# Attention and FFN kernel: whole turns at a unit's end in the last head, edge column and square on ScalarE, key product in score banks, last block closed in halves

## The chip, the cores and the metric

The kernel runs on one core of one Trainium2 chip. The metric is device time in microseconds (us) of one execution. The kernel before was run three times: 1582.94 us in the median, 1581.42 to 1584.07. Engines are named as in the profile: PE (TensorE), DVE (VectorE), ACT (ScalarE), POOL (GpSimd) and SP (SyncE), which here only issues DMAs.

## The reference

The input is x of shape (2, 2048, 256), fp32. There are two stages, each followed by a residual and a layer norm.

```python
q, k, v = x @ Wq + bq, x @ Wk + bk, x @ Wv + bv          # 16 heads of 16, q and k rotated
probs = softmax(q @ k.T / sqrt(16))                      # 2 x 16 heads, 2048 x 2048
x = layernorm(x + probs @ v)

x_prev = x shifted by one token (zero at the start of a sequence)
xr = mu_r * x + (1 - mu_r) * x_prev
xk = mu_k * x + (1 - mu_k) * x_prev
out = sigmoid(xr @ W_r.T) * (square(relu(xk @ W_k.T)) @ W_v.T)
x = layernorm(x + out)
```

## The kernel before, in words

Every engine has its own program, written out by hand; semaphores order them. There is no scheduler: an instruction stands on its engine where the code puts it, and waits there for the semaphore counts that the code names.

**Attention.** The 32 pairs of batch and head (called heads here, 0 to 31) are worked one after the other by `period(h)`, each in 16 units `kt` of 128 keys. In a unit PE writes four score tiles of 128 keys by 512 queries (L543, each as four matmuls of 32 columns) into three PSUM banks `score_ps` used in turn, ACT takes the exponential of each (L696), and at the unit's end PE multiplies the four tiles of the unit before with the values (`pv`, L479) into the bank `pv_ps`. Score tile n waits until the exponential of tile n-3 is done. In the heads before the last, PE also computes the scores of the head after for its maxima (L446), and DVE reduces these (L931). The last head, 31, has no such work beside it.

**Beside the last head.** Three blocks of 512 tokens of batch 0 are prepared for the FFN while head 31 runs: DVE normalises them (`normalise`, L966), PE turns each from tokens to channels (`turn`, 8 transposes of 128 x 128, L491), DVE copies the turned block out of PSUM, sets the edge column for the shift by one token and multiplies with 1 - mu (`take_turned`), and mixes (`mix`, L1003). `project_r(0)` is eight matmuls of 128 x 256 (L503). In `period(LAST)` the iterator `stage_c`, fed by `beside(kt)`, gives one of these PE instructions after each score tile: turns start at units 5, 7 and 14, the r product at unit 10, there after every second tile.

**FFN.** Eight blocks n of 512 tokens. PE's order for a block is: turn of block n+1 (from n = 2 on), `project_r(n)`, `value(n-1)`, `project_key(n)`. PE's first instruction after the last head, `project_key(0)`, stands behind a wait for `pv_turned`, since its second bank is `pv_ps`, which DVE has to read first (`turn_context`, L941). ACT does the turned copy (`take_turned`, L715), the multiplication with 1 - mu (L721), the sigmoid (L727) and the relu (L734). DVE does the edge column (`edge`, L978, or L975 where the sequence starts), the mix, the square of the relu (`square`, L1011), the gating and the residual (`finish`, L1018 and L1021, in two halves), and the statistics (`block_stats`, L957, L960). POOL computes 1/sqrt(variance + eps) (`inverse`, L858, L861) and normalises the output of blocks 0 to 5 (L874); DVE normalises blocks 6 and 7 at the end (L1084), and SP stores each block by one DMA of 512 KB (L401).

The banks: `ring_ps` is two double banks, one for turns (`turn_ps`), one for r (`r_ps`). `key_ps` is `score_ps[2]` and `pv_ps`, `value_ps` is `score_ps[0]` and `score_ps[1]`.

The order around the change is set by DVE's and ACT's in-order programs: the edge column of block n+1 stands on DVE behind the gating, square, statistics and normalisation of the iteration before, ACT's multiplication waits for it, and DVE's mix waits for ACT.

## Time and profile before

| what | value |
|---|---|
| median of three runs | 1582.94 us |
| time of the profiled execution | 1584.12 us |
| its span | 1582.3 us |
| PE busy | 1545.5 us (98%) |
| DVE busy | 1345.3 us (85%) |
| ACT busy | 1139.0 us (72%) |
| POOL busy | 335.3 us (21%) |
| granted PE clock, mean | 0.993 |

The profiled execution took 1584.12 us, its span, from the first to the last instruction, 1582.3 us; 1.8 us lie around the span. The shares are averages over the whole program. The change touches only the last 160 us: the units 5 to 15 of the last head (from 1446.4 us), and the FFN (from 1484.2 us). What it does is read there, from the waits of each engine in order of time.

### The profile page before, as it was taken

Reading aid. Unit: us, or ns where it says so; the run is one execution under the profiler, and the core shown is the slowest. Engines: PE = TensorE matmul, PEld = TensorE weight load, DVE = VectorE, ACT = ScalarE, POOL = GpSimd, SP = SyncE. Lnnn points to the kernel's source line nnn. Section 1 sums busy time; section 2 is a strip of 40 time slices with the busy share of each in tenths; the row PEclk is TensorE's granted clock in tenths of the full one; section 3 lists DMA queues with packets and bytes.
Section 4 is the critical chain, followed back from the end, with each engine's and each line's share of the span. In section 5 each row is a group of like instructions: output and inputs, shape, how many; then the busy total and the mean of one; then the engine's idle time right before and its main releaser. Section 6 shows DMA issues by size and latency. Waiting matters only on the chain. (4 is left out here: it accounts for less than half of the span.)

```text
span 1582.3 us, 47773 instructions
## 1 busy us (share of the span) xinstructions
PE 1545.5 (98%) x21184; PEld 765.5 (48%) x21184; DVE 1345.3 (85%) x1398; ACT 1139.0 (72%) x2187; POOL 335.3 (21%) x327
## 2 busy tenths in 40 slices
PE   5999999999999999999999999999999999999997
PEld 3343445555445544455445444544444455443574
DVE  3447999999999999999999999999999999996577
ACT  3225777777777777777777777777777777778442
POOL 2330322112221322132213221121210000001165
PEclk9999999999999999999999999999999999999999
DMA  6625211121101111121112111211101111000012
GB/s 230 182 73 174 76 22 22 22 76 19 18 15 45 48 22 22 22 75 22 23 22 75 22 22 22 75 22 18 19 16 17 22 22 22 3 2 2 1 41 67
DMA packets 34735, 68.20 MB, mean 43 GB/s; under 512 B 9760, under 2 KB 19744, under 8 KB 32736
## 3 DMA queue, kind: packets, MB, share of 16 engines
q1 hardware_dynamic: 32560, 62.03, 16.0%
q8 instruction: 166, 2.72, 0.7%
q10 hardware_dynamic: 1968, 3.12, 0.5%
q14 instruction: 41, 0.34, 0.1%
HBM read 26.97 MB, written 11.53 MB: 24 GB/s over the span
## 5 line engine op out<-in xcount | busy, mean ns | idle before, releaser
L931 DVE TENSOR_REDUCE tile_max<-ring_ps 128x1 f32<-128x1024 f32 x1024 | 1204.2, 1216 | 164.6 <-PE ring_ps L446 163.5
L696 ACT ACTIVATE probs<-score_ps 128x512 f32<-128x512 f32 x2048 | 1059.6, 603 | 270.6 <-PE score_ps L543 270.1
L446 PE MATMUL ring_ps<-k_stack,q_stack 96*32 96x512 bf16 x8192 | 838.9, 381 | 11.0 <-DMA q_stack<-rope 10.1
L543 PE MATMUL score_ps<-q_stack,k_stack 99*32 99x512 bf16 x8192 | 841.7, 381 | 4.0 <-ACT probs L696 2.9
L479 PE MATMUL pv_ps<-probs,v_aug 128*32 128x512 f32 x4096 | 541.5, 592 | 0.0
L543 PEld LDWEIGHTS score_ps<-q_stack,k_stack 99*32 99x32 bf16 x8192 | 258.8, 96 | 311.7 <-ACT probs L696 146.8
L446 PEld LDWEIGHTS ring_ps<-k_stack,q_stack 96*32 96x32 bf16 x8192 | 253.5, 96 | 309.0 <-DVE tile_max L931 120.5
L479 PEld LDWEIGHTS pv_ps<-probs,v_aug 128*32 128x32 f32 x4096 | 146.7, 111 | 82.7 <-ACT probs L696 1.6
L773 POOL TENSOR_TENSOR neg_cuts<-neg_max,zeros 128x16 bf16<-128x16 f32 x32 | 7.0, 220 | 740.5 <-DVE neg_max L918 740.5
L766 POOL TENSOR_TENSOR v_aug<-v_all,b_v_s 128x256 f32<-128x256 f32 x32 | 23.3, 730 | 281.5 <-PE pv_ps L479 256.1
L425 PE MATMUL score_ps<-xz,w_qk_s 128*128 128x512 f32 x96 | 50.8, 657 | 6.4 <-DMA b_qk_s<-b_qk 6.4
L785 POOL TENSOR_TENSOR ctx_part<-ctx_turn,recip 128x256 f32<-128x256 f32 x32 | 19.8, 620 | 137.0 <-DVE recip L946 137.0
L661 ACT ACTIVATE probs<-score_ps,b_qk_s 128x512 f32<-128x512 f32 x21 | 14.4, 687 | 47.7 <-PE score_ps L425 47.7
L795 POOL TENSOR_TENSOR rope<-rope 128x2048 f32<-128x2048 f32 x7 | 31.9, 4561 | 30.3 <-DMA rope<-qk_raw 30.3
L874 POOL TENSOR_SCALAR xz<-xz,moments,rstd 128x256 f32<-128x256 f32 x24 | 36.8, 1546 | 0.6
L1003 DVE SCALAR_TENSOR_TENSOR rope<-rope,mu_s 128x512 f32<-128x512 f32 x32 | 23.1, 780 | 13.2 <-ACT rope L721 13.2
L503 PE MATMUL ring_ps<-w_rkv_s,rope 128*128 128x256 f32 x128 | 31.2, 388 | 1.5 <-DVE rope L1003 1.5
L425 PEld LDWEIGHTS score_ps<-xz,w_qk_s 128*128 128x128 f32 x96 | 17.8, 204 | 29.8 <-issue 22.5
L796 POOL TENSOR_TENSOR rope<-rope 128x2048 f32<-128x2048 f32 x7 | 32.0, 4569 | 0.0
L802 POOL TENSOR_TENSOR rope<-rope 128x2048 f32<-128x2048 f32 x7 | 31.9, 4558 | 0.1
L721 ACT ACTIVATE rope<-rope,mu_c 128x512 f32<-128x512 f32 x20 | 12.8, 710 | 24.0 <-DVE rope L978 19.3
L592 PE MATMUL score_ps<-w_rkv_s,rope 128*128 128x256 f32 x128 | 29.2, 381 | 0.2
(73 smaller groups left out, 544.6 us busy)
## 6 DMA issues: line engine op xcount, KB each, us to landing
q_stack<-rope SPq DMA_DIRECT2D x186, 64.0 KB, 2.4
k_stack<-rope SPq DMA_DIRECT2D x186, 64.0 KB, 2.4
qk_raw<-probs SPq DMA_DIRECT2D x28, 256.0 KB, 2.5
rope<-qk_raw SPq DMA_DIRECT2D x7, 1024.0 KB, 4.8
rope<-qk_raw SPq DMA_DIRECT2D x14, 512.0 KB, 6.9
xz<-x_ch SPq DMA_DIRECT2D x8, 512.0 KB, 6.7
xz<-x_tok SPq DMA_DIRECT2D x2, 2048.0 KB, 12.9
out<-xz SPq DMA_DIRECT2D x8, 512.0 KB, 2.9
```

Of the source, the lines that this page charges most:

```text
L425: mm = pe.matmul(bank[:, :], w_qk_s[:, c, m:m + P], x_s[:, b, c, t:t + TOK], start=c == 0, stop=c == CHUNKS - 1)
L446: mm = pe.matmul(ring_ps[k % 2][g:g + VCOLS, c * TOK:(c + 1) * TOK], q_stack[0:ROWS, buf, qt * P + g:qt * P + g + VCOLS], k_stack[0:ROWS, ...
L479: mm = pe.matmul(pv_ps[j * VCOLS:(j + 1) * VCOLS, :], v_aug[:, h % 2, kt, :], probs[:, kt % 2, j, :], start=kt == 0, stop=kt == TILES - 1, ...
L503: mm = pe.matmul(r_ps[:, q * DIM:(q + 1) * DIM], mixed[:, n % 2, 0, c, q * P:(q + 1) * P], w_rkv_s[:, 0, c, :], start=c == 0, stop=c == CH ...
L543: mm = pe.matmul(score_ps[n % SCORE_BANKS][g:g + VCOLS, :], k_stack[0:ROWS_M, h % STACKS, kt * P + g:kt * P + g + VCOLS], queries[:, j], s ...
L592: mm = pe.matmul(value_ps[q // 2][:, q % 2 * DIM:(q % 2 + 1) * DIM], key_act[:, n % 2, c, q * P:(q + 1) * P], w_rkv_s[:, 2, c, :], start=c ...
L696: act.activation(probs[:, kt % 2, j, :], score_ps[n % SCORE_BANKS][:, :], ACT.Exp, scale=SCALE).then_inc(exps_done, 1)
L795: pool.tensor_tensor(raw, raw, cos_s, ALU.mult).then_inc(quad_step, 1)
L796: pool.tensor_tensor(swapped, swapped, sin_s, ALU.mult).then_inc(quad_step, 1)
L802: pool.tensor_tensor(raw, raw, swapped, ALU.add).then_inc(quad_step, 1)
L874: ins = pool.tensor_scalar(z_tile(tile), z_tile(tile), moments[:, tile, 0:1], rstd2[:, tile:tile + 1], ALU.subtract, ALU.mult)
L931: dve.reduce_max(tile_max[:, h % 2, unit // 2, unit % 2:unit % 2 + 1], slot[:, :], AX.X)\
```

## The change

Six edits:

1. In the last head the turns are issued whole, all eight transposes after the unit's `pv`; two matmuls of r follow `pv` in each of the units 10 to 13. No more PE instruction stands between score tiles.
2. `key_ps` is now the two score banks before the last one used, `value_ps` the last score bank and `pv_ps`. The wait for `pv_turned` moves from before `project_key(0)` into `value(0)`.
3. From block 3 on the edge column is written by ACT, between the turned copy and the multiplication. ACT's copy waits for the mix two blocks back only, its multiplication for the mix one block back (one buffer of `prev_part`).
4. The square moves from DVE (one instruction of 1024 columns) to ACT (two of 512 with the function Square, each after its relu).
5. DVE's statistics over batch 1 are no longer split around `square(0)`.
6. The last block's reciprocal deviations are computed for two tiles at a time. After the first half's gating and statistics DVE normalises block 6 and computes `shift` = -mean * rstd2; ACT then normalises the first half (Identity with scale and bias) and SP stores it; the second half goes through DVE, and SP stores it by its own DMA.

```diff
-R_CYCLE = 10
+R_CYCLES = (10, 11, 12, 13)
...
-        value_ps = score_ps[0:2]
-        key_ps = (score_ps[2], pv_ps)
+        final = item(LAST, TILES - 1, BLOCKS - 1)
+        key_ps = tuple(score_ps[(final - back) % SCORE_BANKS] for back in (2, 1))
+        value_ps = (score_ps[final % SCORE_BANKS], pv_ps)
...
-            for g in range(A_GROUPS):
+            for g in range(A_GROUPS - 1):
...
+            for half, signal, count in ((0, half_ready, 1), (1, last_ready, A_GROUPS - POOL_OUT)):
+                t = (A_GROUPS - 1) * TPB + 2 * half
+                sp.wait_ge(signal, count)
+                sp.dma_start(out_t[:, t:t + 2, :], z_block(A_GROUPS - 1)[:, 2 * half:2 * half + 2]).then_inc(out_done, DMA)
...
                     pe.wait_ge(ring_freed, RING_CREDIT + RING_TOTAL)
-                    return turn(0)
                 if kt in TURN_CYCLES:
-                    return turn(TURN_CYCLES.index(kt))
-                if kt == R_CYCLE:
-                    return project_r(0)
-                return None
+                    for _ in turn(TURN_CYCLES.index(kt)):
+                        pass
+                if kt in R_CYCLES:
+                    for _ in itertools.islice(first_r, TPB * CHUNKS // len(R_CYCLES)):
+                        pass
...
-                        if h == LAST:
-                            if j == 0:
-                                stage_c = beside(kt) or stage_c
-                            if not R_CYCLE <= kt < TURN_CYCLES[-1] or j % 2:
-                                next(stage_c, None)
...
                         pv(h, kt - 1)
-                for _ in stage_c:
-                    pass
+                    if h == LAST:
+                        beside(kt)
...
             def value(n):
                 pe.wait_ge(key_ready, n + 1)
+                if n == 0:
+                    pe.wait_ge(pv_turned, ALL_HEADS)
...
-                after(pe, relu_ready, n)
+                after(pe, relu_ready, CHUNKS * n)
...
-            pe.wait_ge(pv_turned, ALL_HEADS)
             project_key(0)
...
                 act.wait_ge(y_turned, n + 1)
-                after(act, mixed_ready, n)
+                act.wait_ge(mixed_ready, n - 1)
                 for c in range(CHUNKS):
                     ins = act.copy(y_ch[:, n % 2, c, 1:TOK + 1], turn_ps[:, c * TOK:(c + 1) * TOK])
                 ins.then_inc(y_ch_ready, 1)
+                if n % BLOCKS == 0:
+                    edge = zeros[:, 0:CHUNKS].unsqueeze(2)
+                else:
+                    act.wait_ge(y_ch_ready, n)
+                    edge = y_ch[:, (n + 1) % 2, :, TOK:TOK + 1]
+                act.copy(y_ch[:, n % 2, :, 0:1], edge).then_inc(edge_ready, 1)
                 act.wait_ge(edge_ready, n + 1)
                 act.wait_ge(y_ch_ready, n + 1)
+                act.wait_ge(mixed_ready, n)
...
                 for c, o in enumerate(key_ps):
-                    ins = act.activation(relu[:, c, :], o[:, :], ACT.Relu)
-                ins.then_inc(relu_ready, 1)
+                    act.activation(relu[:, c, :], o[:, :], ACT.Relu).then_inc(relu_ready, 1)
+                after(act, kv_ready, 2 * (n - 1))
+                for c in range(CHUNKS):
+                    act.wait_ge(relu_ready, CHUNKS * n + c + 1)
+                    ins = act.activation(key_act[:, n % 2, c, :], relu[:, c, :], ACT.Square)
+                ins.then_inc(key_ready, 1)
...
+            def finish_half():
+                act.wait_ge(shift_ready, 1)
+                for q in range(2):
+                    tile = (A_GROUPS - 1) * TPB + q
+                    ins = act.activation(z_tile(tile), z_tile(tile), ACT.Identity, bias=shift[:, q:q + 1],
+                                         scale=rstd2[:, tile:tile + 1])
+                ins.then_inc(half_ready, 1)
...
-            def square(n):
-                dve.wait_ge(relu_ready, n + 1)
-                after(dve, kv_ready, 2 * (n - 1))
-                dve.tensor_tensor(key_act[:, n % 2], relu, relu, ALU.mult).then_inc(key_ready, 1)
...
                 if n + 1 < A_GROUPS:
-                    if n > 1:
-                        edge(n + 1)
                     mix(n + 1)
-                if n == A_GROUPS - 1:
-                    square(n)
                 for half in range(2):
                     finish(n - 1, half)
-                if n < A_GROUPS - 1:
-                    square(n)
...
+            first = (A_GROUPS - 1) * TPB
             for half in range(2):
                 finish(A_GROUPS - 1, half)
                 block_stats(A_GROUPS - 1, half)
...
+                if half == 0:
+                    normalise_out(first - TPB, first, A_GROUPS - 1)
+                    normalise_out(first, first + 2, A_GROUPS, shifted=True)
+            normalise_out(first + 2, first + TPB, A_GROUPS + 1)
```

Three places show how the order of instructions changes. The first is PE at the end of the last head, from the end of unit 13: the third turn (into ring_ps, from id and v_all) and unit 15, then the first key product. Before:

```order
L479 MATMUL pv_ps<-probs,v_aug 32x512 x4
L543 MATMUL score_ps<-q_stack,k_stack 32x512 x4
L491 MATMUL ring_ps<-id,v_all 128x128
L543 MATMUL score_ps<-q_stack,k_stack 32x512 x4
L491 MATMUL ring_ps<-id,v_all 128x128
L543 MATMUL score_ps<-q_stack,k_stack 32x512 x4
L491 MATMUL ring_ps<-id,v_all 128x128
L543 MATMUL score_ps<-q_stack,k_stack 32x512 x4
L491 MATMUL ring_ps<-id,v_all 128x128
L479 MATMUL pv_ps<-probs,v_aug 32x512 x8
L603 MATMUL score_ps<-rope,w_rkv_s 128x512 x2
L603 MATMUL pv_ps<-rope,w_rkv_s 128x512 x2
```

The same place after the change, from the last two r matmuls of unit 13:

```order
L512 MATMUL ring_ps<-w_rkv_s,rope 128x256 x2
L553 MATMUL score_ps<-q_stack,k_stack 32x512 x16
L488 MATMUL pv_ps<-probs,v_aug 32x512 x4
L500 MATMUL ring_ps<-id,v_all 128x128 x8
L553 MATMUL score_ps<-q_stack,k_stack 32x512 x16
L488 MATMUL pv_ps<-probs,v_aug 32x512 x8
L613 MATMUL score_ps<-rope,w_rkv_s 128x512 x4
```

The eight transposes stand in one row, behind `pv` and ahead of unit 15's scores; the key product writes score banks only. The second place is ACT in the FFN, here from the relu of one block to that of the next. Before (L734 relu, L715 turned copy, L721 multiplication, L727 sigmoid):

```order
L734 ACTIVATE v_all<-score_ps 128x512
L734 ACTIVATE v_all<-pv_ps 128x512
L715 COPY rope<-ring_ps 128x512 x2
L721 ACTIVATE rope<-rope,mu_c 128x512 x4
L727 ACTIVATE v_all<-ring_ps 128x1024
L734 ACTIVATE v_all<-score_ps 128x512
```

After (L750 relu, L754 square, L724 copy, L731 edge column, L737 multiplication, L743 sigmoid):

```order
L750 ACTIVATE v_all<-score_ps 128x512 x2
L754 ACTIVATE rope<-v_all 128x512 x2
L724 COPY rope<-ring_ps 128x512 x2
L731 COPY rope<-rope 128x2
L737 ACTIVATE rope<-rope,mu_c 128x512 x4
L743 ACTIVATE v_all<-ring_ps 128x1024
```

The square and the edge column came onto ACT, and ACT's order holds one table load between its last exponential and its last activation, before and after alike. The third place is DVE at the end of the program, from the gating of the last block's first half. Before (L1084 is the normalisation of blocks 6 and 7):

```order
L1018 TENSOR_TENSOR rope<-score_ps,v_all 128x512
L1021 TENSOR_TENSOR xz<-rope,v_all 128x2x256
L957 BN_STATS stats<-xz 128x6 x2
L960 BN_AGGR moments<-stats 128x2 x2
L1084 TENSOR_SCALAR xz<-xz,moments,rstd 128x256 x8
```

After:

```order
L1045 TENSOR_TENSOR rope<-score_ps,v_all 128x512
L1048 TENSOR_TENSOR xz<-rope,v_all 128x2x256
L989 BN_STATS stats<-xz 128x6 x2
L992 BN_AGGR moments<-stats 128x2 x2
L1062 TENSOR_SCALAR xz<-xz,moments,rstd 128x256 x4
L1058 SCALAR_TENSOR_TENSOR shift<-moments,rstd 128x2
L1045 TENSOR_TENSOR rope<-pv_ps,v_all 128x512
L1048 TENSOR_TENSOR xz<-rope,v_all 128x2x256
L989 BN_STATS stats<-xz 128x6 x2
L992 BN_AGGR moments<-stats 128x2 x2
L1062 TENSOR_SCALAR xz<-xz,moments,rstd 128x256 x2
```

Block 6's normalisation and the shift now stand ahead of the second half's gating, and two tiles instead of eight stand at the very end. (The piece of before starts at the second half's gating.)

## Rows read from the trace of the kernel before

**Rows 1.** Timeline of PE, unit 4, a plain one: start, us, instruction, idle before.

```profile
1444.14 0.82 PE L543 MATMUL score_ps<-q_stack,k_stack 99*32 99x512 bf16 x12
1445.29 0.40 PE L543 MATMUL score_ps<-q_stack,k_stack 99*32 99x512 bf16 x4 [0.33 <-ACT probs L696]
```

**Rows 2.** Timeline of PE, start of unit 5 (L491 is a transpose).

```profile
1446.38 0.39 PE L543 MATMUL score_ps<-q_stack,k_stack 99*32 99x512 bf16 x4
1446.70 0.33 PE L491 MATMUL ring_ps<-id,v_all 128*128 128x128 f32 x1
1446.96 0.40 PE L543 MATMUL score_ps<-q_stack,k_stack 99*32 99x512 bf16 x4
```

**Rows 3.** Timeline of PE, start of unit 10 (L503 is r).

```profile
1461.87 0.60 PE L543 MATMUL score_ps<-q_stack,k_stack 99*32 99x512 bf16 x8
1462.41 0.70 PE L503 MATMUL ring_ps<-w_rkv_s,rope 128*128 128x256 f32 x2
1463.04 0.62 PE L543 MATMUL score_ps<-q_stack,k_stack 99*32 99x512 bf16 x8
```

**Rows 4.** Timeline of PE, unit 15 to the first key product.

```profile
1478.04 0.40 PE L543 MATMUL score_ps<-q_stack,k_stack 99*32 99x512 bf16 x4
...
1480.39 1.92 PE L479 MATMUL pv_ps<-probs,v_aug 128*32 128x512 f32 x16
1484.24 1.98 PE L603 MATMUL score_ps<-rope,w_rkv_s 128*128 128x512 f32 x4 [1.92 <-DVE ctx_turn L941]
```

**Rows 5.** Timeline of ACT: exponentials of unit 4, then after the last exponential.

```profile
1444.64 2.06 ACT L696 ACTIVATE probs<-score_ps 128x512 f32<-128x512 f32 x4 [0.17 <-PE score_ps L543]
...
1480.87 1.28 ACT L727 ACT_TABLE_LOAD   x1
1482.16 1.03 ACT L727 ACTIVATE v_all<-ring_ps 128x1024 f32<-128x1024 f32 x1
```

**Rows 6.** Timeline of DVE: the third turned block's copy, the mix of block 2.

```profile
1480.50 1.29 DVE L986 COPY rope<-ring_ps 128x512 f32<-128x512 f32 x2 [14.11 <-PE ring_ps L491]
...
1493.57 2.72 DVE L1003 SCALAR_TENSOR_TENSOR rope<-rope,mu_s 128x512 f32<-128x512 f32 x4
```

**Rows 7.** Timeline of PE, turns and later starts in the FFN.

```profile
1498.12 1.04 PE L491 MATMUL ring_ps<-id,v_all 128*128 128x128 f32 x8
1498.99 3.62 PE L503 MATMUL ring_ps<-w_rkv_s,rope 128*128 128x256 f32 x16
...
1509.33 1.04 PE L491 MATMUL ring_ps<-id,v_all 128*128 128x128 f32 x8
...
1558.96 1.96 PE L603 MATMUL score_ps<-rope,w_rkv_s 128*128 128x512 f32 x4 [1.27 <-ACT v_all L734]
```

**Rows 8.** Groups by line, 1484.2 to 1571: count, busy us, mean ns, idle before.

```profile
L721 ACT ACTIVATE rope<-rope,mu_c 128x512 f32<-128x512 f32 x20 | 12.8, 710 | 24.0 <-DVE rope L978 19.3 <-DVE rope L975 4.6
L1003 DVE SCALAR_TENSOR_TENSOR rope<-rope,mu_s 128x512 f32<-128x512 f32 x24 | 17.6, 791 | 13.2 <-ACT rope L721 13.2
L1011 DVE TENSOR_TENSOR rope<-v_all 128x1024 f32<-128x1024 f32 x8 | 9.7, 1217 | 0.9 <-ACT v_all L734 0.9
```

**Rows 9.** Timeline of DVE at the end of the program.

```profile
1571.30 0.69 DVE L1018 TENSOR_TENSOR rope<-score_ps,v_all 128x512 f32<-128x512 f32 x1 [1.90 <-PE score_ps L592]
...
1575.95 1.35 DVE L1084 TENSOR_SCALAR xz<-xz,moments,rstd 128x256 f32<-128x256 f32 x4
1577.55 1.38 DVE L1084 TENSOR_SCALAR xz<-xz,moments,rstd 128x256 f32<-128x256 f32 x4 [0.25 <-POOL rstd L861]
```

**Rows 10.** Timeline of POOL: the power over 16 columns and, last, over 4.

```profile
1494.46 3.28 POOL L861 TENSOR_TENSOR rstd<-rstd,minus_half 128x16 f32<-128x16 f32 x1
...
1576.47 1.05 POOL L861 TENSOR_TENSOR rstd<-rstd,minus_half 128x4 f32<-128x4 f32 x1
```

**Rows 11.** DMA issues: count, KB each, median us to landing.

```profile
qk_raw<-probs SPq DMA_DIRECT2D x28, 256.0 KB, 2.5
out<-xz SPq DMA_DIRECT2D x8, 512.0 KB, 2.9
```

More of the change, by code:

```diff
@@ L1 @@
+import itertools
 from contextlib import ExitStack
@@ L1056, in _ @@
             dve.wait_ge(z_ready, ALL_HEADS)
-            tile_stats(range(TILES, TILES + TILES // 2))
-            square(0)
-            tile_stats(range(TILES + TILES // 2, BATCH * TILES))
+            tile_stats(range(TILES, BATCH * TILES))
             for n in range(1, A_GROUPS):
```

34 lines of the change are left out of this document (24 added, 10 removed).

## The prediction, on record before the changed kernel ran

> **What bounds the kernel now.** I read the page first: PE is busy nearly throughout, but that is an average over 30 heads that the change leaves alone. So I went by stretches, and then by each engine's timeline from the middle of the last head on.
>
> In the last head the bound is a loop between PE and ACT. A unit without side work takes 2.24 us, from 1444.14 to 1446.38 [rows 1, 2]. In it PE's fourth score tile starts 1.15 after the first, having waited 0.33 for an exponential [rows 1]; its four matmuls take 0.23, and then `pv` runs until the unit's end, 0.86. Whatever PE does between the fourth tile and the next unit's first is added to this loop one for one, since ACT has nothing queued then. In the units with side work the loop is stretched. One turn among score tiles makes the step from tile to tile 0.58 (1446.38 to 1446.96 [rows 2]) where the tile alone needs 0.22 (half of a pair, see below): the transpose starts 0.32 after the tile, and the next tile 0.26 after the transpose.
>
> The head ends with PE idle: its last `pv` starts at 1480.39 and takes 1.92, and the first key product comes at 1484.24, released by DVE's reading of `pv_ps` [rows 4]. DVE was late there because it had begun on the third turned block at 1480.50, when the turn spread over units 14 and 15 was done [rows 6].
>
> In the FFN PE starts a new block every 11.21 us while it has work in stock (turn at 1498.12, next turn at 1509.33), which is a turn of 0.87 and three products of 3.45 [rows 7]. Later blocks take longer. The cause is in the groups: ACT's multiplication waits 24.0 us for DVE's edge column, and DVE's mix 13.2 us for ACT's multiplication [rows 8]. The two hand the block to each other, and PE waits for the mix.
>
> **The change part by part.** All sums are against the profiled execution; its time is 1584.12, 1.18 above the median of 1582.94, so I take the difference off the median.
>
> *Units 5 to 14.* Before they take 1478.04 - 1446.38 = 31.66 [rows 2, 4]. After there are three units with a whole turn, four with two r matmuls, and three plain ones. A whole turn is 0.87 [rows 7]. To it comes the price of switching PE from score tiling to full tiles and back. In rows 2 the score to turn to score step is 0.58; less the tile's 0.22 and one transpose's 0.11 (an eighth of 0.87) that leaves 0.25. So a turn unit is 2.24 + 0.87 + 0.25 = 3.36. Two r matmuls are a quarter of 3.45, 0.86; a pair of tiles takes 0.54 with the switch in, the r matmul 0.63 until the next tile [rows 3], which leaves 0.1 + 0.2 for the switch, so 2.24 + 0.86 + 0.28 = 3.38. Sum: 3 x 3.36 + 4 x 3.38 + 3 x 2.24 = 30.3, a gain of 1.4. It all comes from the turns; the r units lose 0.15 each against 3.23 before (units 10 to 14 take 16.17, from 1461.87 to 1478.04 [rows 3, 4], 3.23 each). The bounds: ACT's slack in a unit (0.17 before each unit's four exponentials [rows 5]) hides that much of each of the seven insertions, gain 2.6; or a turn costs what its eight single transposes would, 8 x 0.36 = 2.9 instead of 1.12, a loss of 3.9. I take 1.4, as the switch is seen once per insertion in the nearest rows.
>
> *Unit 15 and the way out.* Before, unit 15 and the two `pv` take 4.27, then 1.92 idle: 6.20 from 1478.04 to 1484.24 [rows 4]. After, the tiles stand alone: fourth tile at 1.15, first `pv` 1.38 to 2.24, second `pv` to 3.10, with its last part just behind the last exponential (ACT starts 0.5 into a unit, at 1444.64, and takes 2.06 [rows 5]: 2.56). The key product needs nothing of `pv_ps` now, so it starts at 3.2 to 3.3: gain 2.95, first key product at 1484.24 - 1.4 - 2.95 = 1479.9. What is late next: r of block 1 at 1483.3 needs ACT's sigmoid of block 0, which is the table load 1.28 and 1.03 [rows 5] after the last exponential at about 1479.3, so 1481.6. The value product at 1486.8 needs relu and squares (3.5 after 1479.9, plus 2.4), 1485.8, and DVE's reading of `pv_ps` (about 1481). The third turn is done at 1476.8 instead of 1480.4, so DVE's copy and multiplication are through by 1480. Then come 16 tiles of statistics and the mix of block 2, wanted by PE at 1494.6; before, the mix ended at 1496.3 [rows 6], 12.1 after that reading, now without the 1.22 of the square [rows 8], so near 1492. All are covered, the narrowest by 1 us.
>
> *The FFN's blocks.* From the first key product to the half of the last value product PE took 1571.28 - 1484.24 = 87.04 (the DVE row at 1571.30 starts on it [rows 4, 9]). PE's own work on that way is 3.45 (key 0), 3 x 3.45 (block 1), 5 x 11.21 (blocks 2 to 6), 3 x 3.45 and 1.73 to the half, 81.9, and 0.2 for the first fill. One wait stays: two key products stand next to each other at the end, and the second waits for ACT's relu of the first, 1.27 [rows 7]. That makes 83.4: a gain of 3.6, if the hand-over no longer paces PE. From the end of a key product: relu 1.1 (the 1.27 for which PE waits on just these two [rows 7], less the releases), squares. The square is not in the trace on ACT; the nearest row is L721, 128x512 from SBUF, 710 ns [rows 8], so two with their waits take 1.3 (0.6 at the least, if they ran like half of DVE's 1217 ns; 2.6 if twice as long). Turned copy 1.1, edge column 0.3 (DVE's copy of two columns is 0.16; 0.1 to 0.6), four multiplications 2.56, releases 0.3: 6.7. Mix 2.9. So the mix ends 9.6 after the key product, and PE wants it after the next block's turn, three products and its own turn's 0.87, at 12.1. Slack 2.5; the bounds above eat 1.6 of it. ACT's whole block is this 6.7 and the sigmoid 1.0, 7.7 of 11.21. DVE's is 2.9 + 2.7 + 1.7 + 1.35 = 8.7. Bounds of this term: 0 to 4.9 (if the 1.27 vanished too). I take 3.6.
>
> *The end.* Before, DVE needs 7.63 from its gating at 1571.30 to 1578.93, of which each half's gating and statistics 2.33, POOL's round trip 1.6 less what the normalisation of block 6 covers, and the last four tiles 1.38 [rows 9]. After: first half 2.3, block 6's four tiles 1.35 (in cover of POOL's round trip for two columns), shift 0.15, second half 2.4, POOL 1.2, two tiles 0.7: 8.1. POOL's power takes 3.28 for 16 columns and 1.05 for 4 [rows 10], 0.19 a column, so 0.7 for two. That is 0.5 later. The last DMA carries 256 KB: 2.5 us by the store of that size against 2.9 for 512 KB [rows 11], 0.4 earlier. ACT's half (two activations after the shift, 1.4, and a DMA of 2.5) lands before the second half is issued. Net 0.1 later; bounds 0.4 earlier (the power's saving doubled) to 1.2 later (no saving in POOL or DMA). I take 0.
>
> Sum: 1.4 + 2.95 + 3.6 = 8.0 less. **Forecast 1582.94 - 8.0 = 1574.9 us** (the profiled execution: 1576.1).
>
> **The rivals.** *A: the hand-over still paces the blocks.* If ACT's string after the key product is 3.2 us longer than I make it (the slack of 2.5, and 0.7 on each of five blocks), the 3.6 are not gained; time 1578.5. For it: before, PE waited on just this mix. Against it: the DVE work between (1.22 square, 2.7 gating, 1.7 statistics, 1.35 normalisation) no longer stands between a relu and the next edge column.
>
> *B: the switch of tiling at a unit's end is dear.* Now it falls behind `pv`, which is fp32 in four column tiles, and before the score tiles on which ACT waits; [rows 2] show the switch beside bf16 score tiles only. Price: seven insertions times (c - 0.26). From c = 0.46 on the gain of 1.4 in units 5 to 14 has become a loss; at c = 1.0 the time is 1580.1. **Slower than before** by 0.2% it is from c = 0.26 + 11.2 / 7 = 1.85: all seven unit ends would stand nearly as long as a plain unit; at c = 2 the time is 1587. Against it: `pv` changes to score tiles and back in every plain unit with no gap beyond the 0.33 that ACT causes [rows 1]. The Trainium skill ("TensorEngine Tiling (Array Packing)", Key Properties) states that changing the tiling mode drains TensorE, and gives no price; by that rule the interleaved order was the dear one.
>
> *C: table loads.* If Square were not in the sigmoid's table, each block would need two more loads: 2 x 1.28 [rows 5] = 2.6, just the slack, so 1575 to 1576. The Trainium skill ("ScalarE: Activation LUTs", Table sets: the hidden batching unit) names relu, copy, identity and abs as being in every set and does not name Square, and puts a switch at 1.28 + 1.38 us. An estimate by that page is 5.3 a block, 2.8 over the slack on five blocks: 1589, slower. Against it: ACT's order holds a single table load after the last exponential; and before the sigmoid the trace shows only 1.28 from the exponential to the activation [rows 5].
>
> *D: the head doesn't pay.* The turn insertions reach their bound (2.9 each): 1574.9 + 5.3 = 1580.2.
>
> **How the numbers follow.** My case 0.77, A 0.12, B 0.04 (half of it slower), C 0.03 (a third slower), D 0.04. What a measurement of this kernel can tell from no change is 0.2%, 3.2 us. Within it (above 1579.8) fall D and half of B: 0.06. Slower 0.03. Faster 0.91. The range for 8 in 10 runs from 1572.5 (the head's 1.2 more, the wait of 1.27 gone) to 1578.9 (A, and the end 0.4 later).
>
> **What would show it.** PE's timeline after: units 5, 7, 14 at 3.36 and 10 to 13 at 3.38, plain ones at 2.24; first key product near 1480, with no wait for DVE; turns 11.2 apart from block 2 to the end; a wait of 1.3 before the last key product alone; the last value product's half at 1563.3; DVE's end 8.1 later. On ACT one table load, squares of 0.6 to 0.7 each, and the mix released by ACT about 2.5 before PE asks for it. Wrong it is if turns stay 12.5 apart (A), if unit ends stand idle on PE (B, D), or if DVE's statistics of 16 tiles hold up r of block 2.

## The result and the profile after

The changed kernel takes 1576.0 us in the median of five runs (1573.42 to 1577.16), the kernel before, run beside it, 1583.3 (1581.42 to 1584.54, five runs). The ratio is 0.995, its 95% interval 0.9935 to 0.9964: faster by 7.3 us, and by more than the 0.2% that a measurement of this kernel can tell. The forecast was 1574.9, range 1572.5 to 1578.9. The profiled execution took 1576.04 us, its span is 1574.2 (before: 1582.3).

The page's line of busy times of after:

```profile
PE 1539.2 (98%) x21184; PEld 749.2 (48%) x21184; DVE 1335.9 (85%) x1384; ACT 1147.3 (73%) x2210; POOL 335.6 (21%) x329
```

The shares say nothing: PE is at 98% as before. Part of the 8.1 us between the spans isn't the change's either. To see that, take a point up to which both programs are the same. DVE's only instruction on `mu_c` is one. It stands in DVE's timeline (start, duration, engine and line, names and shapes) at

```profile
1429.22 0.16 DVE L1038 TENSOR_SCALAR mu_c<-mu_s 128x4 f32<-128x4 f32 x1
```

in before, and in after at

```profile
1428.60 0.16 DVE L1077 TENSOR_SCALAR mu_c<-mu_s 128x4 f32<-128x4 f32 x1
```

Here 0.62 us are already gained, in code that nobody touched. From this anchor to the span's end before takes 153.08 and after 145.60: the change brings **7.48 us**. Every experiment below is read in this way, "from the anchor to the end", beside its timed median. Each kernel has one such trace; where two kernels have the same code, their stretches agree to 0.03 us: from the anchor to the first key product 51.23 to 51.26 in the six with the changed head (after, e3, e5, e6, e7, e10), and from there to DVE's first gating of the last block 83.72 or 83.73 in nine (after, e1, e2, e6 to e11).

The 7.48 us by stages (the last value half is taken, as in the prediction, 0.02 ahead of DVE's gating of it):

| stage | before | after | gain | forecast of after |
|---|---|---|---|---|
| units 5 to 14 | 31.66 [rows 2, 4] | 30.49 | 1.17 | 30.3 |
| unit 15 to the first key product | 6.20 [rows 4] | 3.61 | 2.59 | 3.25 |
| first key product to the last value half | 87.04 [rows 4, 9] | 83.71 | 3.33 | 83.4 |
| from there to the end of the span | 7.63 + 3.37 [rows 9] | 8.08 + 2.53 | 0.39 | 0 |

**The units.** PE's timeline of after, from unit 5's first tile to unit 6's, and the start of unit 10's side work. In brackets stand the idle time before an instruction and what ended it:

```profile
1445.76 0.82 PE L553 MATMUL score_ps<-q_stack,k_stack 99*32 99x512 bf16 x12
1446.91 0.40 PE L553 MATMUL score_ps<-q_stack,k_stack 99*32 99x512 bf16 x4 [0.33 <-ACT probs L705]
1447.14 1.03 PE L488 MATMUL pv_ps<-probs,v_aug 128*32 128x512 f32 x8
1448.10 1.09 PE L500 MATMUL ring_ps<-id,v_all 128*128 128x128 f32 x8
1449.13 0.83 PE L553 MATMUL score_ps<-q_stack,k_stack 99*32 99x512 bf16 x12
...
1461.57 1.13 PE L512 MATMUL ring_ps<-w_rkv_s,rope 128*128 128x256 f32 x4
1462.63 0.83 PE L553 MATMUL score_ps<-q_stack,k_stack 99*32 99x512 bf16 x12
```

Against [rows 2] the eight transposes stand in one piece. They need 1449.13 - 1448.10 = 1.03 until the next tile, and `pv` before them 0.96 instead of its 0.86, where PE goes from four column tiles of 32 to the full width: 0.10 before and 0.16 behind the 0.87 of the transposes. Unit 5 is 3.37 long. The r matmuls take 1.06 (of which they themselves 0.86) and the same 0.10 ahead, unit 10 is 3.41. And `[0.33 <-ACT probs L705]` is still there: each unit with side work waits for the exponential as a plain one does. The work at the unit's end is paid in full.

**The way out of the head,** PE's timeline:

```profile
1476.25 0.83 PE L553 MATMUL score_ps<-q_stack,k_stack 99*32 99x512 bf16 x12
...
1477.64 2.29 PE L488 MATMUL pv_ps<-probs,v_aug 128*32 128x512 f32 x16
1479.86 3.70 PE L613 MATMUL score_ps<-rope,w_rkv_s 128*128 128x512 f32 x8
```

and ACT's:

```profile
1476.76 2.07 ACT L705 ACTIVATE probs<-score_ps 128x512 f32<-128x512 f32 x4 [1.31 <-PE score_ps L553]
1478.85 1.28 ACT L743 ACT_TABLE_LOAD   x1
1480.14 1.02 ACT L743 ACTIVATE v_all<-ring_ps 128x1024 f32<-128x1024 f32 x1
```

The 1.92 us of idle PE of [rows 4] are gone: the key product follows `pv` without a wait. But the last of `pv`'s matmuls needs the last exponential, which ends at 1476.76 + 2.07 = 1478.83, and the key product comes 1.03 later, where I had put about 0.7 (3.25 less 2.56). A `pv` is four matmuls, one for each score tile, each on a column tile of its own and each two records. PE's timeline at two moments of the second `pv`, 1478.80 and 1479.10, lists what runs just then:

```profile
1478.50 0.60 PE L488 MATMUL pv_ps<-probs,v_aug 128*32 128x512 f32 x3
```

```profile
1478.88 0.65 PE L488 MATMUL pv_ps<-probs,v_aug 128*32 128x512 f32 x4
```

Three of the four matmuls start at 1478.50, the fourth only at 1478.88, behind the last exponential (the other three records of the second line are the second ones of the three matmuls above).

**A block of the FFN,** ACT's timeline from the key product of block 2 on:

```profile
1505.15 1.09 ACT L750 ACTIVATE v_all<-score_ps 128x512 f32<-128x512 f32 x2 [4.53 <-PE score_ps L613]
1506.12 1.15 ACT L754 ACTIVATE rope<-v_all 128x512 f32<-128x512 f32 x2
1507.16 1.08 ACT L724 COPY rope<-ring_ps 128x512 f32<-128x512 f32 x2
1508.11 0.22 ACT L731 COPY rope<-zeros 128x2 f32<-128x2 f32 x1
1508.36 2.56 ACT L737 ACTIVATE rope<-rope,mu_c 128x512 f32<-128x512 f32 x4
```

Not one wait stands between the relu and the last multiplication. The groups by line from 1479.8 to 1563.6 (count, busy us, mean ns, idle before), beside the 24.0 us and the 13.2 us of [rows 8]:

```profile
L737 ACT ACTIVATE rope<-rope,mu_c 128x512 f32<-128x512 f32 x20 | 12.8, 712 | 0.2
L1035 DVE SCALAR_TENSOR_TENSOR rope<-rope,mu_s 128x512 f32<-128x512 f32 x24 | 17.5, 788 | 14.1 <-ACT rope L737 14.1
```

ACT's 24.0 us of waiting have become 0.2, while DVE's wait for ACT has even grown, from 13.2 to 14.1, and costs nothing: what matters is when the mix is done. In DVE's timeline it starts at

```profile
1510.96 3.06 DVE L1035 SCALAR_TENSOR_TENSOR rope<-rope,mu_s 128x512 f32<-128x512 f32 x4 [2.67 <-ACT rope L737]
```

and is done at 1514.0, and PE asks for it at 1517.04, 3.0 later. So PE's turns stand 11.22 apart to the end (1493.73, 1504.95 and so on to 1538.60), and the one wait left in the FFN is that of the last key product for ACT's relu, 1.27 as in [rows 7].

**The end,** DVE's timeline, and under it POOL's:

```profile
1563.59 0.69 DVE L1045 TENSOR_TENSOR rope<-score_ps,v_all 128x512 f32<-128x512 f32 x1 [2.03 <-PE score_ps L602]
...
1565.92 1.35 DVE L1062 TENSOR_SCALAR xz<-xz,moments,rstd 128x256 f32<-128x256 f32 x4
...
1567.42 0.69 DVE L1045 TENSOR_TENSOR rope<-pv_ps,v_all 128x512 f32<-128x512 f32 x1
...
1570.93 0.74 DVE L1062 TENSOR_SCALAR xz<-xz,moments,rstd 128x256 f32<-128x256 f32 x2 [1.08 <-POOL rstd L891]
```

```profile
1566.44 0.88 POOL L891 TENSOR_TENSOR rstd<-rstd,minus_half 128x2 f32<-128x2 f32 x1
...
1570.20 0.69 POOL L891 TENSOR_TENSOR rstd<-rstd,minus_half 128x2 f32<-128x2 f32 x1
```

DVE ends 8.08 after its first gating instead of 7.63, since block 6's four tiles (1.35) now stand ahead of the second half. The span ends 2.53 later instead of 3.37: half the bytes, and more saved than the 0.4 that I had taken.

### The profile page after: what moved, and what is told of

It reads as the page before. It is cut to its first block, busy times and chain, and to the rows that moved or that the text cites. A ratio compares the mean times of both kernels' runs of the same rounds, so it can differ in the third digit from the quotient of the medians.

```text
span 1574.2 us, 47785 instructions
## 1 busy us (share of the span) xinstructions
PE 1539.2 (98%) x21184; PEld 749.2 (48%) x21184; DVE 1335.9 (85%) x1384; ACT 1147.3 (73%) x2210; POOL 335.6 (21%) x329
## 3 DMA queue, kind: packets, MB, share of 16 engines
q8 instruction: 166, 2.72, 0.7%
## 4 chain that ended last, share of the span: by engine, by line
PE 96%; ACT 1%; DMA 1%; SPq 1%; DVE 1%; issue 0%; POOL 0%; ACTq 0%; POOLq 0%; DVEq 0%
PE ring_ps L455 29%; PE score_ps L553 28%; PE pv_ps L488 28%; PE score_ps L434 3%; PE ring_ps L512 2%; PE score_ps L613 2%; PE score_ps L602 1%; PE pv_ps L434 1%; PE pv_ps L602 1%; PE score_ps L443 1%; ACT probs L705 1%; PE ring_ps L500 0%; SPq L320 0%; SPq L316 0%; DMA b_qk_s<-b_qk 0%; DMA rope<-rope 0%
## 5 line engine op out<-in xcount | busy, mean ns | idle before, releaser
L705 ACT ACTIVATE probs<-score_ps 128x512 f32<-128x512 f32 x2048 | 1058.0, 602 | 270.5 <-PE score_ps L553 270.2
L553 PEld LDWEIGHTS score_ps<-q_stack,k_stack 99*32 99x32 bf16 x8192 | 251.5, 96 | 323.0 <-ACT probs L705 145.8
L455 PEld LDWEIGHTS ring_ps<-k_stack,q_stack 96*32 96x32 bf16 x8192 | 246.8, 96 | 315.1 <-DVE tile_max L963 115.9
L1035 DVE SCALAR_TENSOR_TENSOR rope<-rope,mu_s 128x512 f32<-128x512 f32 x32 | 23.0, 778 | 14.2 <-ACT rope L737 14.1
L750 ACT ACTIVATE v_all<-score_ps 128x512 f32<-128x512 f32 x16 | 8.7, 595 | 33.8 <-PE score_ps L613 33.8
L613 PE MATMUL score_ps<-rope,w_rkv_s 128*128 128x512 f32 x64 | 28.9, 595 | 1.3 <-ACT v_all L750 1.3
## 6 DMA issues: line engine op xcount, KB each, us to landing
xz<-x_tok SPq DMA_DIRECT2D x2, 2048.0 KB, 12.5
```

The lines of the kernel that those rows point to most:

```text
L455: mm = pe.matmul(ring_ps[k % 2][g:g + VCOLS, c * TOK:(c + 1) * TOK], q_stack[0:ROWS, buf, qt * P + g:qt * P + g + VCOLS], k_stack[0:ROWS, ...
L553: mm = pe.matmul(score_ps[n % SCORE_BANKS][g:g + VCOLS, :], k_stack[0:ROWS_M, h % STACKS, kt * P + g:kt * P + g + VCOLS], queries[:, j], s ...
L613: mm = pe.matmul(o[:, :], w_rkv_s[:, 1, c, m * P:(m + 1) * P], mixed[:, n % 2, 1, c, :], start=c == 0, stop=c == CHUNKS - 1)
L705: act.activation(probs[:, kt % 2, j, :], score_ps[n % SCORE_BANKS][:, :], ACT.Exp, scale=SCALE).then_inc(exps_done, 1)
```

## The experiments

Eleven kernels ran. Four undo a part of the changed kernel, one puts a single part on the kernel before, two split a pair of parts, four try what the traces point to. The table has the timed ratios to the kernel before, and the time from the anchor to the end, which resolves a few tenths.

| run | median (runs) | ratio to before, 95% | anchor to end | against after |
|---|---|---|---|---|
| after | 1576.0 (5) | 0.995, 0.9935 to 0.9964 | 145.60 | |
| e1 turns spread again | 1578.7 (6) | 0.9969, 0.9958 to 0.998 | 147.38 | +1.78 |
| e2 first key product waits again | 1577.17 (5) | 0.9956, 0.9944 to 0.9969 | 146.49 | +0.89 |
| e3 edge and square on DVE again | 1578.0 (9) | 0.9967, 0.9958 to 0.9977 | 149.24 | +3.64 |
| e5 square alone on DVE | 1576.36 (4) | 0.9954, 0.9941 to 0.9967 | 145.88 | +0.28 |
| e6 edge alone on DVE | 1575.41 (4) | 0.995, 0.9937 to 0.9963 | 145.60 | 0.00 |
| e7 the old end | 1577.28 (6) | 0.9957, 0.9945 to 0.9969 | 146.01 | +0.41 |
| e4 before, with edit 2 alone | 1581.09 (11) | 0.9987, 0.9978 to 0.9996 | 152.50 | (before - 0.58) |
| e8 `pv` before the fourth tile | 1573.2 (5) | 0.9936, 0.9923 to 0.9948 | 144.84 | -0.76 |
| e9 side work before the fourth tile | 1570.68 (5) | 0.9918, 0.9904 to 0.9932 | 142.01 | -3.59 |
| e10 another order at the end | 1572.98 (5) | 0.9938, 0.9925 to 0.995 | 144.25 | -1.35 |
| e11 e9 and e10 | 1571.37 (5) | 0.9922, 0.9909 to 0.9934 | 140.67 | -4.93 |

**e1: edit 1 undone.**

```diff
                 if kt in TURN_CYCLES:
-                    for _ in turn(TURN_CYCLES.index(kt)):
-                        pass
+                    return turn(TURN_CYCLES.index(kt))
...
+                        if h == LAST:
+                            if j == 0:
+                                stage_c = beside(kt) or stage_c
+                            if not R_CYCLE <= kt < TURN_CYCLES[-1] or j % 2:
+                                next(stage_c, None)
```

> The changed kernel with edit 1 alone undone: one transpose or r matmul after each score tile, as before. My theory: units 5 to 14 go back from 30.5 to 31.7 us, and the way from unit 15 to the first key product from 3.6 to 4.3 (only PE's own work, no wait for DVE), so the first key product comes 1.9 later than in the changed kernel, near 1481.8; the FFN's blocks stay bound by PE (83.7 from there to the last value product's half). Time 1576.0 + 1.9 = 1577.9 us. Rival (the way out is the banks' doing alone): units give 1.2 back and nothing else, 1577.2. Second rival: DVE, late again with the third turned block, holds up r of block 2, and the time is 1579 or more.

Measured +1.78. PE's timeline of e1 at the way out (unit 15 starts at 1478.91):

```profile
1478.91 0.40 PE L552 MATMUL score_ps<-q_stack,k_stack 99*32 99x512 bf16 x4
...
1483.13 2.41 PE L614 MATMUL score_ps<-rope,w_rkv_s 128*128 128x512 f32 x5
```

From unit 15 to the key product it takes 4.22 where after takes 3.61. So whole turns save 1.16 in units 5 to 14 and 0.61 here: taken off the changed kernel, edit 1 is worth 1.8 of the 7.5 us. The second rival of the expectation is out: from the key product to DVE's gating e1 takes 83.72, as after does.

**e2: edit 2 undone.**

```diff
-        key_ps = tuple(score_ps[(final - back) % SCORE_BANKS] for back in (2, 1))
-        value_ps = (score_ps[final % SCORE_BANKS], pv_ps)
+        value_ps = score_ps[0:2]
+        key_ps = (score_ps[2], pv_ps)
...
+            pe.wait_ge(pv_turned, ALL_HEADS)
             project_key(0)
```

> The changed kernel with edit 2 alone undone: key product in score bank 2 and pv_ps, and the wait for DVE's reading of pv_ps before it. My theory: in the changed kernel DVE reads pv_ps at once (1479.96 to 1480.68), so the wait that comes back is 0.85 and not the 1.92 of before; first key product near 1480.7, the rest unchanged, 1576.0 + 0.85 = 1576.9 us. Rival: the wait comes back whole, since it was the bank that made it: 1577.9.

Measured +0.89. PE's timeline of e2 shows the one wait that comes back, shorter than the 1.92 of [rows 4], since DVE is done with the third turned block when `pv` ends:

```profile
1478.82 1.55 PE L610 MATMUL score_ps<-rope,w_rkv_s 128*128 128x512 f32 x3 [0.81 <-DVE ctx_turn L971]
```

Edits 1 and 2 share the gain on the way out: the way out takes 4.49 with edit 1 and without 2 (e2), 4.2 with edit 2 and without 1 (e1, e4), 3.61 with both, 6.20 with neither.

**e4: edit 2 alone on the kernel before** (the same lines the other way round).

> The kernel before with edit 2 alone done: key product in score banks, the wait for pv_turned moved to the first value product. My theory: the first key product comes 1.9 earlier, but DVE's string of the FFN starts when it did, and it paces the later blocks; PE only waits longer for the mix. Time as before, 1583.3, within 0.3 us. Rival (a wait removed from PE is a gain): 1.9 us less, 1581.4.

Only 0.58 is left at the end, more than the 0.3 of the expectation, far less than the rival's 1.9. The timed interval (0.6 to 3.5 us faster) can't tell, the trace does. PE's timeline of e4:

```profile
1482.02 3.70 PE L606 MATMUL score_ps<-rope,w_rkv_s 128*128 128x512 f32 x8
...
1490.27 1.99 PE L595 MATMUL score_ps<-w_rkv_s,rope 128*128 128x256 f32 x8 [1.09 <-DVE rope L1013]
```

The key product comes 2.0 earlier from the anchor than before (53.02 against 55.02), but the value product waits for DVE's square, which stands behind the first half of batch 1's statistics, and these behind DVE's reading of `pv_ps`, which is no earlier. By the turn of block 3 (1497.26 here, 1498.12 in before [rows 7]) 0.64 is left. The wait was moved, not removed. Two other runs show what lets edit 2 pay. e1 has the same spread turns, and the key product at the same place (53.01 from the anchor), with edits 3 to 5 in: there the value product waits for nothing. e3 has whole turns and the square on DVE: there DVE reads `pv_ps` at 51.34 from the anchor (54.25 in before and e4), its first square ends at 1487.27, and the value product starts at 1487.32, only 0.14 later than behind r without a wait. So either edit 1 or edits 3 to 5 are enough at this place. That is why the parts' own gains don't sum in any order.

**e3: edits 3, 4 and 5 undone.**

```diff
-                act.wait_ge(mixed_ready, n - 1)
+                act.wait_ge(mixed_ready, n)
...
-                act.copy(y_ch[:, n % 2, :, 0:1], edge).then_inc(edge_ready, 1)
...
-                    ins = act.activation(key_act[:, n % 2, c, :], relu[:, c, :], ACT.Square)
-                ins.then_inc(key_ready, 1)
...
+            def square(n):
+                dve.wait_ge(relu_ready, CHUNKS * (n + 1))
+                after(dve, kv_ready, 2 * (n - 1))
+                dve.tensor_tensor(key_act[:, n % 2], relu, relu, ALU.mult).then_inc(key_ready, 1)
...
+                    if n > 1:
+                        edge(n + 1)
                     mix(n + 1)
```

> The changed kernel with edits 3, 4 and 5 undone: edge column and square on DVE again, statistics split around the first square. My theory: the blocks are paced by the DVE-ACT string again, 12.5 apart from the third on, and the string starts 3.5 earlier than before (statistics of batch 1 from 1482.5 instead of 1486.0), so the last value product's half comes 3.5 earlier than before, 4.2 later than in the changed kernel: 1576.0 + 4.2 = 1580.2 us. Rival (the gains are a sum of independent terms): the blocks give back just their 3.3, 1579.3. Second rival: the hand-over was never the cause and the blocks stay at 11.2: 1576.0.

Measured +3.64. The 4.2 of the expectation was reckoned without the anchor and had the 0.62 ahead of it in it; 3.6 is left of it, and the rival that adds up independent terms had 3.3. The blocks are slow again. Timelines of e3, PE, ACT and DVE:

```profile
1530.53 3.72 PE L512 MATMUL ring_ps<-w_rkv_s,rope 128*128 128x256 f32 x16 [0.68 <-DVE rope L1023]
```

```profile
1512.50 2.56 ACT L730 ACTIVATE rope<-rope,mu_c 128x512 f32<-128x512 f32 x4 [4.71 <-DVE rope L995]
```

```profile
1502.65 3.00 DVE L1023 SCALAR_TENSOR_TENSOR rope<-rope,mu_s 128x512 f32<-128x512 f32 x4 [2.63 <-ACT rope L730]
...
1512.39 0.06 DVE L995 MEMSET rope<- 128x2 f32 x1
1515.09 2.88 DVE L1023 SCALAR_TENSOR_TENSOR rope<-rope,mu_s 128x512 f32<-128x512 f32 x4 [2.64 <-ACT rope L730]
```

This is a closed ring of two engines: mix, gating, square (1.22, at 1508.22), statistics, normalisation, edge (all DVE, 1502.65 to 1512.45, with no wait among them), ACT's multiplication (2.6), next mix. Its period is 1515.09 - 1502.65 = 12.44, and PE's r starts stand 12.5 apart, against PE's own 11.21.

**e5 and e6: only the square, only the edge column back on DVE** (e3's lines, one half each; e5 also splits the statistics around the first square again, which is edit 5 undone).

> The changed kernel with the square alone back on DVE (the edge column stays on ACT). My theory: what paced the blocks was a closed string, in which DVE's edge column stood behind its square, statistics and normalisation and ACT waited for it; one cut is enough. ACT's multiplication then starts some 2.5 us after a key product, the mix ends before PE asks for it, turns stay 11.2 apart, and the last value product's half comes where it does in the changed kernel (117.8 after unit 5's start), within 0.2 (the first square stands among DVE's statistics). Time 1576.1 us. Rival: the square's 1.2 us on DVE is a term of its own on the way, a good half of the 3.7 of the experiment with both, 1578.

> The changed kernel with the edge column alone back on DVE (the square stays on ACT). My theory: DVE's edge column comes at its place behind the normalisation, about 3.65 us after a key product, where ACT's multiplication starts at 3.4 in the changed kernel; the delay of 0.25 is within the slack of 2.5. Turns 11.2 apart, last half at 117.8 after unit 5's start, 1576.0 us. Rival: the wait of ACT for DVE is what costs, not the square, and most of the 3.7 comes back, 1578 to 1579.

Measured +0.28 and 0.00: each edit alone does what both do. The reason is the ring. In e6 ACT and DVE show

```profile
1506.68 2.56 ACT L730 ACTIVATE rope<-rope,mu_c 128x512 f32<-128x512 f32 x4 [0.44 <-DVE rope L1000]
```

```profile
1497.97 3.00 DVE L1028 SCALAR_TENSOR_TENSOR rope<-rope,mu_s 128x512 f32<-128x512 f32 x4 [2.63 <-ACT rope L730]
...
1509.27 2.88 DVE L1028 SCALAR_TENSOR_TENSOR rope<-rope,mu_s 128x512 f32<-128x512 f32 x4 [2.64 <-ACT rope L730]
```

The ring is still closed, but without the square its period is 11.30, just PE's 11.21; the 0.09 a block is paid out of the stock with which the first blocks start. In e5 the ring is open (ACT writes the edge column itself) and the square (1.23) lies in DVE's free time. Of e5's 0.28, 0.24 arise at the value product of block 0: behind DVE's first square it starts 3.59 after r instead of 3.46, and it takes 0.11 longer. Undone together they close the ring at 12.44. The 3.6 us belong to neither edit, and the load of DVE or ACT alone was not the bound.

**e7: edit 6 undone** (one store of 512 KB, one power of four columns, no half on ACT).

```diff
-                if half == 0:
-                    normalise_out(first - TPB, first, A_GROUPS - 1)
-                    normalise_out(first, first + 2, A_GROUPS, shifted=True)
-            normalise_out(first + 2, first + TPB, A_GROUPS + 1)
+            normalise_out(first - TPB, first, A_GROUPS - 1)
+            normalise_out(first, first + TPB, A_GROUPS)
```

> The changed kernel with edit 6 alone undone: last block normalised whole on DVE after block 6, stored by one DMA of 512 KB. My theory: DVE's end goes back from 8.08 to 7.63 after its first half's gating, and the way from there to the end of the span from 2.5 to 3.4, so 0.4 later in all, 1576.4 us. Rival: a store that starts early is worth its whole difference, 0.85, 1576.9. Second rival: the end is worth nothing, 1576.0.

Measured +0.41, and DVE's end is that of before, 7.63 from the gating, then 3.4 to the span's end. Edit 6 brings 0.4. Its weak point is the order: block 6's tiles (1.35) stand between the halves.

**e8: `pv` and the side work before the fourth score tile,** units 2 to 15. The idea was that the wait of 0.33 for the exponential would be filled in every unit.

```diff
                     for j in range(BLOCKS):
+                        if h == LAST and kt > 1 and j == BLOCKS - 1:
+                            pv(h, kt - 1)
+                            beside(kt)
                         n = item(h, kt, j)
```

> The changed kernel with, in units 2 to 15 of the last head, pv and the turn or r matmuls issued between the third and the fourth score tile instead of after the fourth. My theory: the loop of PE and ACT is what paces a unit, and PE waits there 0.33 for an exponential; with pv in that place a plain unit is bound by ACT's four exponentials, 2.06 instead of 2.24, a turn unit by PE's own work, 2.87 instead of 3.37, an r unit 2.9 instead of 3.41: 6 x 0.18 + 3 x 0.5 + 4 x 0.51 = 4.6 less, the way out as it is (the last exponential still sets it), 1571.4 us. Rival: the fourth tile comes too late for ACT and the unit is as long as before, 1576. Second rival: the head is shorter, but DVE's string is late for r of block 2 and takes it back.

Wrong: -0.76 instead of -4.6. PE's timeline of e8:

```profile
1445.16 1.09 PE L500 MATMUL ring_ps<-id,v_all 128*128 128x128 f32 x8
1446.18 0.83 PE L556 MATMUL score_ps<-q_stack,k_stack 99*32 99x512 bf16 x12
1447.29 0.40 PE L556 MATMUL score_ps<-q_stack,k_stack 99*32 99x512 bf16 x4 [0.27 <-ACT probs L707]
```

The row of twelve behind the turn is now the fourth tile of one unit and the first two of the next, and the wait sits at the tile behind it. There are three score banks and one place per unit where PE leaves the score tiles; putting all that PE does elsewhere at that one place only rotates the cycle. A turn unit takes 3.31 here, 3.37 in after; the wait is 0.27 instead of 0.33, and thirteen units with 0.06 less each make the 0.76.

**e9: only the side work before the fourth tile,** `pv` stays at the unit's end. Now there are two places: three tiles, turn, fourth tile, `pv`.

```diff
                     for j in range(BLOCKS):
+                        if h == LAST and j == BLOCKS - 1:
+                            beside(kt)
                         n = item(h, kt, j)
...
                         pv(h, kt - 1)
-                    if h == LAST:
-                        beside(kt)
```

> The changed kernel with the turn or the two r matmuls issued between the third and the fourth score tile of their unit; pv stays after the fourth. My theory, corrected by the experiment before: the loop has three tiles in flight and PE waits for an exponential before the fourth, wherever pv stands; side work must stand ahead of that wait, apart from pv. Then the 0.33 of waiting and a part of the exponential's time are filled, and a unit with side work is bound by PE's own 2.87 instead of 3.37 to 3.41: 7 x 0.5 = 3.5 less from the anchor (DVE's first instruction on mu, 1428.60) to the end, 142.1 instead of 145.6; 1572.5 us. Rival (the loop only turns, as with pv): 0 to 0.8 less, 1575.5. Second rival: ACT runs dry before the fourth tile and the unit gets longer, 1577.

Measured -3.59. PE's timeline of e9:

```profile
1444.45 0.82 PE L555 MATMUL score_ps<-q_stack,k_stack 99*32 99x512 bf16 x12
1445.20 1.09 PE L500 MATMUL ring_ps<-id,v_all 128*128 128x128 f32 x8
1446.22 0.40 PE L555 MATMUL score_ps<-q_stack,k_stack 99*32 99x512 bf16 x4
1446.45 1.04 PE L488 MATMUL pv_ps<-probs,v_aug 128*32 128x512 f32 x8
1447.31 0.82 PE L555 MATMUL score_ps<-q_stack,k_stack 99*32 99x512 bf16 x12
```

The fourth tile has no wait: the turn covers the 0.33, and ACT works on the three tiles in stock meanwhile. A turn unit takes 2.86, an r unit (1456.89 to 1459.79) 2.90, each 0.51 less; seven of them are 3.57. This is the version of the last head that the traces point to.

**e10: another order at the end.** ACT normalises block 6, DVE does both halves of block 7 back to back.

```diff
+            normalise_out(first - TPB, first, A_GROUPS - 1, shifted=True)
             for half in range(2):
...
-                if half == 0:
-                    normalise_out(first - TPB, first, A_GROUPS - 1)
-                    normalise_out(first, first + 2, A_GROUPS, shifted=True)
+            normalise_out(first, first + 2, A_GROUPS, shifted=True)
             normalise_out(first + 2, first + TPB, A_GROUPS + 1)
```

> The changed kernel with another order at the end: block 6 is normalised by ACT (its shift computed by DVE before the last block's first gating), DVE goes from the first half straight to the second, and the first half's shift follows. My theory: DVE's way from its gating to its end is two halves of 2.33, POOL's round trip for two columns 1.2 and two tiles 0.7, so 6.6 instead of 8.1; the last store is as before. 1.5 less from the anchor to the end, 144.1; 1574.5 us. Rival: ACT's six tiles or two stores at once hold up the last store, and nothing or less than 0.5 is gained, 1575.7.

Measured -1.35. DVE's timeline of e10:

```profile
1564.33 0.69 DVE L1047 TENSOR_TENSOR rope<-score_ps,v_all 128x512 f32<-128x512 f32 x1 [0.44 <-PE score_ps L602]
...
1566.67 0.67 DVE L1047 TENSOR_TENSOR rope<-pv_ps,v_all 128x512 f32<-128x512 f32 x1
...
1570.15 0.73 DVE L1065 TENSOR_SCALAR xz<-xz,moments,rstd 128x256 f32<-128x256 f32 x2 [1.03 <-POOL rstd L893]
```

The second gating starts 2.34 after the first instead of 3.83, and DVE ends after 6.55 instead of 8.08, 1.53 less. From there to the end of the span it takes 2.72 instead of 2.53, which leaves 1.35. The last two stores now stand closer together; whether that is the cause of the 0.19 no run shows.

**e11: e9 and e10 together.**

> Both of the edits before together on the changed kernel. My theory: they act at different places (the last head, the end) and PE's own work sets the time between them, so the gains add: 145.6 - 3.5 - 1.5 = 140.6 from the anchor to the end, 1571.0 us, some 13 less than the kernel before. Rival: with the head 3.5 shorter DVE's statistics and mix of block 2 are late for r, and part of the head's gain is lost: 1572 to 1573.

Measured -4.93, the sum of the two (3.59 + 1.35 = 4.94): stages that follow each other add. Its median, 1571.37, can't be told from e9's 1570.68, whose interval overlaps; from the anchor it is 1.34 faster (more on such medians in the last section). Both beat the changed kernel (ratios to before of 0.9922 and 0.9918 against 0.995; the intervals just don't meet).

## Why the prediction was right, by its own steps

- **Units 5 to 14: right.** The turn unit was forecast at 3.36 and is 3.37, the r unit at 3.38 and is 3.41, the plain one 2.24; the term is 1.17 against 1.4. The switch of tiling, read from [rows 2, 3] as 0.25 and 0.28, is 0.26 and 0.31 at a unit's end. Rival B (a dear switch behind `pv`) and D (transposes that cost the same in one piece) are out. The upper bound, ACT's slack, was not touched, since in this order the slack lies where PE has nothing to put; e9 shows what it takes to use it.
- **Unit 15 and the way out: the mechanism right, the size off.** This is the term that was mis-sized: 3.61 instead of 3.25. I had the second `pv` at its pace in the row, its last part "just behind the last exponential". In the trace the last exponential ends 2.58 after unit 15's start (2.56 forecast), and the key product comes 1.03 behind it. The fourth matmul of this `pv` can't begin sooner, and alone it takes as long as four side by side: 0.98 from its start at 1478.88 to the key product, where a whole `pv` takes 0.96 up to a turn. So 2.59 instead of 2.95.
- **What is late next: right.** Nothing holds up r of block 1, the value product or r of block 2. e4 shows that this was not given: on the kernel before, with the turns spread and the square on DVE, the same earlier key product runs into the square.
- **The FFN's blocks: right.** 3.33 against 3.6 gained; no wait on a mix in PE's timeline, the 1.27 at the end stays. The slack is 3.0, not 2.5: two squares take 1.15 on ACT (1.3 forecast), the edge column 0.22 (0.3). Rival A is out for the changed kernel, and e3 shows it alive when both edits are undone. What I had not seen is that the two edits are substitutes; my reason against A, that DVE's work no longer stands between a relu and the next edge column, holds for edit 3 alone, and edit 4 alone comes to the same by making the ring shorter.
- **Table loads: right.** One load after the last exponential, squares and relus after it with none. Rival C is out. The Trainium skill ("ScalarE: Activation LUTs", What ACT_TABLE_LOAD costs) puts a switch at 1.28 + 1.38 us. The trace agrees on 1.28 and shows no second part: the last exponential ends at 1478.83, the sigmoid starts at 1480.14. The Trainium skill ("ScalarE: Activation LUTs", Table sets: the hidden batching unit) does not name Square among the functions of every set; here Square ran in all eight blocks beside sigmoid and relu with the one load.
- **The end: 0.39 gained where I took 0,** inside the bounds. DVE's 8.08 is as forecast (8.1), what follows it was 0.8 shorter instead of 0.4.

The sum was 8.0, the traces show 7.48 from the anchor. The profiled execution was forecast at 1576.1 and took 1576.04, but 0.62 of that comes from ahead of the anchor and has nothing to do with the reasons: a hit of this closeness is partly luck.

## What to carry to other kernels

When two engines hand a buffer to each other, write down the closed ring of what they do between two hand-overs and compare its period with the pace of the engine that should set the time: opening the ring and shortening it are alternatives, and a wait removed ahead of it mostly moves (e4: 0.58 left of 2.0). In a loop with few banks, side work costs least at the place where the engine waits for a bank anyway, but only if the rest of its other work stays elsewhere (e9), or else the wait rotates along (e8). And compare the stages of two traces from the last instruction at which the programs are still the same.

## What the runs showed of the hardware

Most of the spread between executions arises ahead of the changed part. Over before, after and the eleven experiments the anchor lies between 1426.56 (e8) and 1430.53 (e11), though all instructions ahead of it are the same. PE stands idle for 10 us near the start, until DMAs bring `q_stack`, and the granted clock behind it is 0.50, the 1.2 GHz level. When it comes back to 2.4 GHz differs. Two stretches of e8, with PE's busy time, the other engines', the granted clock (the third figure from the right), the share of the DMA engines and GB/s:

```profile
40.00:44.00 4.00, 3.02 (x11) 1.18 (x12) 1.23 (x1) 0.00 (x0) 0.00 (x0) 0.50 0.05 12
44.00:48.00 4.00, 4.00 (x23) 1.08 (x21) 1.23 (x1) 1.06 (x2) 0.00 (x0) 0.95 0.27 82
```

and the second of them in e11:

```profile
44.00:48.00 4.00, 4.00 (x14) 1.14 (x13) 1.01 (x1) 0.69 (x1) 0.00 (x0) 0.65 0.11 42
```

From 44 to 48 us PE issues 23 matmuls in one and 14 in the other. This puts the second maximum on DVE 1.2 us later (45.73 and 46.99); from 50 to 1431 us DVE's waits for PE's scores of the maxima sum to 149.8 and 153.2 us, and these 3.4 more cover the other 2.7 between the anchors. Why the clock returns at different times, and where those waits arise, stays open.

The anchor goes with the mean granted clock of the whole execution: in the five profiled executions at 0.995 (e2, e6, e7, e8, e9) it lies from 1426.56 to 1427.29, in the eight at 0.992 to 0.994 from 1428.60 to 1430.53. The timed executions of one kernel part in the same way: of e3 the four at 0.993 took 1579.56 to 1580.6 us, the five at 0.995 1577.31 to 1578.0. So a median of few executions depends on how many of each it holds. At 0.995 alone after took 1573.42 and 1573.99 (so e3 is some 3.7 slower, as from the anchor), e9 1569.93 to 1571.13 and e11 1568.74.

Small prices, PE's at a granted clock of 1.00 (2.4 GHz): leaving the 32-column tiling and coming back 0.26 to 0.31 us; a square of 512 fp32 columns on ACT 0.63, two in a row 1.15, against 1.22 for 1024 on DVE; POOL's power of two columns 0.69 to 0.88; from DVE's end to the span's end 2.53 to 2.58 behind a store of 256 KB (2.72 in e10 and e11) and 3.37 to 3.39 behind one of 512 KB; one fp32 `pv` matmul of 512 columns on a column tile of 32, alone, 0.98 to the next product, four side by side 0.96.
